# Products with the identity between the tiles of a hybrid attention and expert kernel: items with a bank of their own, or work in the bank the next item claims

## What is computed

```
x = x + attn_a(layernorm(x))   # 16 heads; groups of 64 rows, local keys + 64 cluster keys
x = x + ffn(layernorm(x))      # router, top-1 of 8 experts, y * max(probs)
x = x + attn_b(layernorm(x))   # 64 landmarks: kernel1 @ iterative_inv(kernel2) @ (kernel3 @ v)
x = x + ffn(layernorm(x))

def iterative_inv(K, n_iter=6):
    V = jnp.swapaxes(K, -1, -2) / denom
    for _ in range(n_iter):
        KV = K @ V
        V = 0.25 * V @ (13.0 * I - KV @ (15.0 * I - KV @ (7.0 * I - KV)))
    return V
```

## Time and profile before

| what | value |
|---|---|
| median of 3 runs | 1086.68 us (1081.27 to 1087.15) |
| profiled execution: span from its first to its last instruction | 1121.9 us |
| what lies around the span in that execution | not shown; span against the median of the runs: 35.2 us more |
| mean granted TensorE clock | 0.925 of full |
| TensorE busy / weight loads | 933.2 us (83%) / 666.9 us (59%) |
| VectorE, ScalarE, GpSimd busy | 831.1 (74%), 641.6 (57%), 472.3 us (42%) |

### The profile page before, as it was taken

How to read it: one execution, slowest core, us unless ns; L and a number is a source line. 1 busy time by engine, 2 the same in 40 slices (tenths; PEclk the granted TensorE clock), 3 DMA queues, 4 the chain that set the end, 5 groups by cost and what they waited for, 6 DMA issues and landing times. The chain is left out here.

```text
span 1121.9 us, 37263 instructions
## 1 busy us (share of the span) xinstructions
PE 933.2 (83%) x15213; PEld 666.9 (59%) x15213; DVE 831.1 (74%) x2089; ACT 641.6 (57%) x1387; POOL 472.3 (42%) x443
## 2 busy tenths in 40 slices
PE   7899989998989888677888986597689989772898
PEld 5567667675766665456566665454466666552653
DVE  3899899888557996567776687878487898685556
ACT  2456656782664574456667585356376776382630
POOL 2355345227356630445524156512543454446421
PEclk8899989999999999888999998689789999895999
DMA  9700000002321100120101101100311110102533
GB/s 319 254 3 3 4 2 3 3 3 95 115 72 58 31 8 13 38 68 12 49 21 52 41 12 35 30 29 2 102 42 50 39 46 20 49 26 90 160 105 99
DMA packets 51079, 61.71 MB, mean 55 GB/s; under 512 B 5601, under 2 KB 46177, under 8 KB 50913
## 3 DMA queue, kind: packets, MB, share of 16 engines
q1 hardware_dynamic: 43584, 42.51, 11.8%
q0 software_dynamic: 5760, 15.74, 4.4%
q10 hardware_dynamic: 1568, 1.09, 0.3%
HBM read 29.70 MB, written 29.62 MB: 53 GB/s over the span
## 5 line engine op out<-in xcount | busy, mean ns | idle before, releaser
L764 POOL TENSOR_TENSOR a_pr<-a_pr,a_smax 128x512 f32<-128x512 f32 x128 | 133.3, 1042 | 177.5 <-DVE a_smax L877 168.0
L1267 POOL TENSOR_TENSOR b_tm<-b_aw,b_sq 128x640 f32<-128x640 f32 (+1 forms) x48 | 65.4, 1362 | 148.9 <-ACT b_sq L1505 143.5
L871 DVE TENSOR_TENSOR a_pr<-a_bank,a_mask 128x512 f32<-128x512 f32 x128 | 82.8, 682 | 42.0 <-PE a_bank L1066 34.7
L963 ACT ACTIVATE a_pr<-a_pr 128x512 f32<-128x512 f32 x128 | 78.6, 630 | 51.9 <-POOL a_pr L764 44.1
L1247 POOL TENSOR_TENSOR b_pa<-b_pa,b_amax 128x512 f32<-128x512 f32 x64 | 67.1, 1048 | 70.3 <-ACT b_pa L1470 61.8
L969 ACT ACTIVATE a_pT<-a_bank 128x512 f32<-128x512 f32 x128 | 71.1, 596 | 41.2 <-PE a_bank L1075 30.0
L1075 PE MATMUL a_bank<-ident,a_pr 128*128 128x128 f32 x512 | 76.4, 289 | 20.2 <-ACT a_pr L963 17.6
L1256 POOL TENSOR_TENSOR b_pa<-b_pa,b_asum 128x512 f32<-128x512 f32 x64 | 66.7, 1043 | 58.4 <-DVE b_asum L1371 54.2
L307 POOL DMA_INDIRECT rows_sorted<-f_rows,f_pos x60 | 58.2, 969 | 72.2 <-DVE f_pos L403 53.8
L1398 DVE SCALAR_TENSOR_TENSOR b_aw<-b_tm,b_inverse 128x320 f32<-128x320 f32 (+1 forms) x144 | 63.4, 440 | 33.1 <-PE b_inverse L1646 13.7
L318 POOL DMA_INDIRECT f_rows<-results_sorted,f_pos x60 | 58.6, 977 | 66.9 <-issue 34.4
(11 more groups left out here) (238 smaller groups left out, 2359.8 us busy)
## 6 DMA issues: line engine op xcount, KB each, us to landing
f_xg<-rows_sorted SPq DMA_DIRECT2D x42, 256.0 KB, 3.2
results_sorted<-f_yg SPq DMA_DIRECT2D x42, 256.0 KB, 2.3
rows_sorted<-f_yg SPq DMA_DIRECT2D x2, 2944.0 KB, 18.5
X<-in_x SPq DMA_DIRECT2D x7, 512.0 KB, 11.0
out<-X SPq DMA_DIRECT2D x7, 512.0 KB
experts_w<-in_e_wT SPq DMA_DIRECT2D x2, 1024.0 KB, 9.3
rows_sorted<-f_rows,f_pos POOLq DMA_INDIRECT x60
f_rows<-results_sorted,f_pos POOLq DMA_INDIRECT x60
```

The source lines that it names most:

```text
L764: nc.gpsimd.tensor_tensor(out=pr[:, u % AHEAD], in0=pr[:, u % AHEAD], in1=smax[:, u % AHEAD, :].unsqueeze(2).broadcast_to([P, HQ, KEYS]), ...
L871: pre.emptied(V_.tensor_tensor(out=pr[:, u % AHEAD], in0=gb[:].rearrange("p (h k) -> p h k", h=HQ), in1=mask[:, u // 4, :].unsqueeze(1).br ...
L963: nc.scalar.activation(pr[:, u % AHEAD], pr[:, u % AHEAD], ACT.Exp, scale=float(HD) ** -0.5)\
L1267: nc.gpsimd.tensor_tensor(out=tm[:, a:b, k], in0=aw3[:, a:b, k], in1=sq[:, a:b, k], op=ALU.subtract).then_inc(s_tm, 1)
```

## The change

The 24 idle items leave both tables. In 91 places of the TensorE lists (28 and 63) stands a new item `warmN_name` instead, with N from 1 to 47, 424 products in all (143 and 281). It is no item of the ring: it claims the bank that the item `name` will claim and issues N products of the identity with itself into it, with no semaphore. `name` stands right behind it or, in places, a few items later (`3.warm7_ta3 3.R3.0 ... 3.ta3`). Everything else keeps its order, but since the idle items took places in the ring, nearly every item now gets another bank. The ring's turns had also kept apart some reads and writes that no semaphore did; seven waits are written out for them.

```
+def warm(nc, pe, ring, n, item, ident):
+    count, name = item[4:].split("_", 1)
+    gb = ring.claim(pe, n, name)
+    for _ in range(int(count)):
+        nc.tensor.matmul(gb[:, 0:P], ident[:], ident[:], start=True, stop=True)
...
 def claimed(entries, experts):
     for n, x in entries:
+        if x.startswith("warm"):
+            continue
...
                 elif item == "xn":                      # VectorE, first attention
+                    if n > 0:
+                        pre.filled_bank(dve, n - 1, "xT1")
+                        pre.filled_bank(dve, n - 1, "xb")
...
                 elif item in ("v0", "v1"):              # VectorE
+                    wait_later(dve, s_pv, (n - 1) * UNITS)
...
                 elif item.startswith("norm"):           # VectorE
+                    if n * NT + t >= 2:
+                        pre.filled_bank(dve, (n * NT + t - 2) // NT, f"yT{(t - 2) % NT}")
...
                 elif item in ("k0", "k1"):              # ScalarE
+                    if n >= 2:
+                        pre.filled_bank(act, n - 2, f"score{UNITS - 1}")
...
                 elif item == "vcl":                     # ScalarE
+                    wait_later(act, s_pv, (n - 1) * UNITS)
...
             def body(item, n, par):                     # TensorE, both attentions
+                if item.startswith("warm"):
+                    warm(nc, pe, pre, n, item, ident)
+                    return
...
-                if item.startswith("idle"):
-                    pre.filled(mm(gb[:, 0:P], ident[:], ident[:], start=True, stop=True), n, item)
-                    mm(gb[:, 0:P], ident[:], ident[:], start=True, stop=True)
-                    pre.emptied(mm(gb[:, 0:P], ident[:], ident[:], start=True, stop=True), n, item)
-                    return
...
                 elif item in ("v0", "v1"):              # TensorE, both attentions
+                    pre.brought_out(pe, n, ["xT0", "xT1"], item)
...
                 elif item == "xn":                      # VectorE, second attention
+                    if n > 0:
+                        ring.filled_bank(dve, n - 1, "xT1")
...
                 elif item == "d":                       # TensorE, second attention
+                    pe.wait_ge(s_k2, (n + 1) * 7)
...
 CLUSTER_ORDER = {
     "pe": """
-        0.idle0 0.idle1 1.idle0 0.xT0 0.xT1 1.idle1 0.lc 2.idle0 0.q0 0.k0 0.k1 0.wT 0.q1 0.xb 0.v0 0.xbT 0.ckv 0.v1
+        0.warm47_xT0 0.xT0 0.xT1 0.warm2_lc 0.lc 0.q0 0.k0 0.k1 0.wT 0.q1 0.warm1_xb 0.xb 0.v0 0.xbT 0.warm3_ckv
```

More of the change, by code:

```diff
@@ L1518, in body @@
             def body(item, n, par):
+                if item.startswith("warm"):
+                    warm(nc, pe, either, n, item, ident)
+                    return
                 if isinstance(n, str):
@@ L1523, in body @@
                 last = None
-                if item.startswith("idle"):
-                    ring.filled(mm(gb[:, 0:P], ident[:], ident[:], start=True, stop=True), n, item)
-                    mm(gb[:, 0:P], ident[:], ident[:], start=True, stop=True)
-                    ring.emptied(mm(gb[:, 0:P], ident[:], ident[:], start=True, stop=True), n, item)
-                    return
                 if item[:2] == "xT":
@@ L1542, in body @@
                 elif item in ("v0", "v1"):
+                    ring.brought_out(pe, n, ["xT0", "xT1"], item)
                     for j in range(2):
@@ new lines @@
+        m0.rx3.0 5.xbT m0.lt2 m0.rx3.1 4.weigh8 4.weigh9 4.weigh10 m0.lg3 4.weigh11 m0.lt3 4.yT1 5.ckv 5.v1 4.turn12
+        4.turn13 4.turn14 4.turn15 4.weigh12 4.weigh13 4.weigh14 4.weigh15 m0.s2 6.xT0 6.xT1 5.score0 6.lc 6.q0 6.k0
+        6.k1 4.pj1 4.yT2 m0.cT 6.wT 4.pj2 6.q1 6.xb 4.yT3 m0.warm1_bi0 m0.bi0 5.turn0 6.v0 6.xbT m0.bi1 4.pj3 6.ckv
+        6.v1 5.turn1 5.turn2 5.score4 5.turn3 m0.tt0 5.weigh0 5.weigh1 5.weigh2 5.weigh3 m0.tt1 m0.ty0 m0.tt2 m0.ty1
+        m0.ty2 m0.tt3 m0.tt4 5.turn4 5.turn5 5.turn6 m0.tt5 m0.ty3 m0.ty4 5.score8 m0.tt6 5.turn7 m0.ty5 m0.tt7
@@ new lines @@
+        0.sc4 0.warm13_sa0 0.sa0 0.tc4 0.tc5 1.q0 1.k0 0.w4 0.w5 0.tc6 0.tc7 0.w6 0.w7 1.warm2_q1 0.R0.0 1.q1 1.k1
+        1.v0 1.v1 1.S20 1.S21 1.S22 1.warm1_sc0 1.sc0 0.ta0 0.warm6_ta1 0.ta1 0.warm2_ta2 0.N0.0 0.ta2 1.S23 1.tc0
+        1.tc1 0.sa4 0.R1.0 1.w0 1.w1 m1.tt0 m1.tt1 m1.ty0 1.tc2 1.tc3 1.kT 1.warm1_sc4 0.N1.0 1.sc4 1.w2 1.d 0.R2.0
+        2.xT0 0.N2.0 1.tc4 1.w3 2.xT1 1.w4 1.tc5 m1.tt2 m1.ty1 0.R3.0 m1.tt3 0.ta3 1.tc6 1.w5 1.A 1.tc7 0.N3.0 0.ta4
+        1.w6 1.w7 0.R4.0 0.ta5 0.ta6 m1.tt4 0.N4.0 1.sa0 0.warm1_ta7 0.R5.0 0.ta7 m1.ty2 m1.ty3 0.N5.0 m1.ty4 0.Z
@@ new lines @@
+        5.sc4 m2.warm4_tt2 4.N1.0 m2.tt2 m2.ty0 m2.ty1 m2.tt3 m2.tt4 4.R2.0 5.tc4 m2.ty2 5.tc5 4.ta3 6.xT0 6.xT1
+        m2.tt5 5.w4 5.w5 4.N2.0 4.ta4 4.ta5 m2.ty3 4.R3.0 4.ta6 5.sa0 5.warm1_tc6 4.N3.0 5.tc6 m2.ty4 m2.tt6 5.kT 5.d
+        4.R4.0 m2.tt7 m2.ty5 4.ta7 4.N4.0 m2.ty6 5.A 4.R5.0 m2.tt8 m2.tt9 5.tc7 m2.ty7 m2.ty8 m2.tt10 4.N5.0 5.w6
+        5.w7 4.Z 5.R0.0 4.sv0 4.sv1 m2.tt11 5.ta0 4.pj0 4.pj1 4.pj2 4.pj3 6.q0 6.k0 6.q1 6.k1 6.v0 5.ta1 5.ta2 6.sc0
+        5.N0.0 m2.ty9 m2.ty10 m2.ty11 m2.tt12 5.R1.0 5.sa4 6.v1 5.N1.0 6.S20 6.S21 6.S22 6.tc0 m2.tt13 6.tc1 m2.ty12
@@ new lines @@
+        m2.tt14 5.R2.0 6.w0 6.w1 6.tc2 6.tc3 6.sc4 m2.warm4_ty13 5.N2.0 m2.ty13 m2.ty14 6.w2 6.w3 m2.tt15 6.tc4 6.tc5
+        6.S23 5.R3.0 5.ta3 m2.tt16 6.w4 6.w5 m2.tt17 m2.ty15 5.ta4 5.ta5 5.ta6 5.N3.0 6.kT 6.sa0 6.warm1_tc6 5.R4.0
+        6.tc6 m2.ty16 6.d 5.N4.0 m2.ty17 6.tc7 5.warm1_ta7 5.R5.0 5.ta7 6.A 6.w6 6.w7 m2.warm1_tt18 5.N5.0 m2.tt18
+        m2.tt19 m2.tt20 5.warm2_Z 5.Z 6.R0.0 m2.bi0 5.sv0 5.sv1 6.ta0 6.ta1 6.N0.0 6.ta2 m2.ty18 6.warm1_sa4 6.R1.0
+        6.sa4 m2.ty19 m2.tt21 6.N1.0 m2.tt22 5.pj0 5.pj1 7.xT0 6.R2.0 m2.bi1 7.xT1 5.pj2 5.pj3 6.N2.0 7.q0 6.R3.0
```

147 lines of the change are left out of this document (69 added, 78 removed).

## The result

The changed kernel takes 1088.8 us (median of 20 runs, 1085.9 to 1092.8), the kernel before 1084.5 (20 runs, 1073.8 to 1090.9): ratio 1.0058, interval 1.0035 to 1.008. It is slower, by 4.3 us in the medians and 6.3 by the ratio, where I had forecast 6.5 us faster. The profiled execution took 1088.86 us.

A forecast was written before the change was run, and what follows sets the result against it. No engine was always busy; whichever of TensorE (83%) and VectorE (74%) was behind set the end. Terms 0.9 + 2.5 - 4.2 - 4.0 - 0.7 - 1.0 = -6.5 us, applied to the median, gave 1080 us, range 1069 to 1093.

The forecast's parts named there:

- Removed ... I cost it at nothing: Taking out 24 idle items (72 products, 16 us of TensorE's time) costs nothing; what it could give is at most 1 us.
- Term 1, the start: 47 products before the first transposes delay the first projection to 16.6 to 17.6 us; cost 0.8 to 1.9, taken as 0.9.
- Term 2, groups without a gap: Products in blocks 2, 3, 7 and the last inverse, among others, that no wait covers; cost 0 to 7.4 us, taken as 2.5.
- Term 3, the hand-over: From block 3 to 4, Z, sv and three pj run at full clock; gain 0 to 4.6 us, taken as 4.2.
- Terms 4 to 6: Half-clock time going: five stretches gain 4.0 us, those at 36.5 and 159.4 us 0.7, two inverses 1.0.
- VectorE takes it back: Rival: TensorE's waits grow by the time freed, half the hand-over gain remains; sum +1.3, put at 1086 us, chance 0.27.
- TensorE's busy time up by little: Sign expected across the kernel: products fill what matmuls at half clock took before, so TensorE's busy time hardly rises.
- The slower rival: Products get stuck beside indirect DMAs in the last inverse, deciding from about 0.4 us each; +7.4, 1094 us, chance 0.16.
- The added waits: Each waits for something that happened long before in the trace, so they cost nothing unless such a lead is eaten up.
- the late signals: Delays beside indirect DMAs at 798 to 811, 964 to 972 and 1022.52 to 1032.23 us; no term was said to rest there.
- term 6: Two inverses at 698.7 and 1012.7 us lose half-clock time; gain 0 to 4 us, taken as 1.0.
- the fast rival: TensorE is behind nearly everywhere, so the half-clock gains reach their upper ends; -18.4 us, 1068 us, chance 0.17.

The follow-up runs named there:

- f2: Kernel before without its 24 idle items, each item's bank as in the changed kernel, no added waits or products; ratio 1.0029.
- f3: Kernel before with its 72 idle products cut from 128 columns to 1, banks, waits and order kept; ratio 1.0036.
- e1: Changed kernel with all 91 groups of products taken out, idle items still gone, new waits in; ratio to the kernel before 1.0037.
- h5: Kernel before with added waits, no new products, and without the 12 idle items of the first stage; ratio 1.0059.
- f1: Kernel before with the added waits alone, idle items, banks and order as before, no new products; ratio 1.0011.
- h4: Kernel before with added waits; second stage as in the changed kernel (its 12 idle items gone, 281 products in); ratio 1.0021.
- g3: Kernel before with idle items kept, added waits, and the 281 products of the second stage alone; ratio 0.9974.
- h6: Kernel before with idle items kept, added waits, and only the 212 second-stage products that have a gap; ratio 0.9967, 1080.2 us.
- e2: Changed kernel without the 47 products at the start alone; ratio to the kernel before 1.0082.
- h1: Kernel before with idle items kept, added waits, and the 47 products at the start alone; ratio 1.0079.
- e3: Changed kernel without the groups that have no gap to fill, 95 products less; ratio to the kernel before 1.0033.
- h2: Kernel before with idle items kept, added waits, and only the 26 first-stage products that have no gap; ratio 1.0051.
- g4: Kernel before with idle items kept, added waits, and 23 products alone at the hand-over from block 3 to block 4; ratio 0.997.
- g1: Kernel before with idle items kept, added waits, and only the 282 of 424 products that have a gap; ratio 0.9972.
- f4: Changed kernel, with its 424 products and waits, with the 24 idle items put back where they stood; ratio to the kernel before 1.004.

## Why the prediction was wrong

**The step that failed first: "Removed ... I cost it at nothing".** I had bounded it at 1 us. The 24 idle items are worth 3 to 4 us by f2, f3 and e1, each with an interval of about 3.5 to either side (h5 for the first stage alone 6, 5 against f1). I had looked at whether they stood in gaps and whether a bank was waited for. What they gave was clock; at which places is argued and not shown: the kernel before has them at 163, 383 to 391 and 415 us, and two of the changed kernel's half-clock stretches (171.1 to 177.9, 420.2 to 423.6) begin a few us behind such a place. f3 shows that it was their work, since it changes nothing but the columns (ratio 1.0036, 1.0004 to 1.0069). And that their 144 records move the edges of the program blocks I did not know.

**The unforeseen term: a halt for instructions, +5.5 us in the profile.** Inserted instructions can cost more than their duration. They moved an edge of a program block into N5 of block 1, on the chain of the inverse, with half clock behind it (18.1 against 12.6 us). That this stretch loses time by the halt is well supported: the lost time stands in nine profiles with the halt and in none of eleven without. What it is worth in the time of the kernel is not shown: h4 has it and is 5 us behind g3, which has not, but h6 has it too (16.6 us) and is the fastest of all. A kernel that only shifts the edges, with nothing else changed, was not run.

**Term 1, the start: mechanism right, size off.** Transposes at 14.95 and first projection at 17.39 lie in the ranges given. But I took 0.9 us, near the low end, and against the same profile it is 1.65. In that profile the clock rose at 16.0; in the second it rose at 13.1 and the projections began at 14.55, so the price is 2.8 at the first projection and 2.3 at score4; alone, beside the idle items, 5.5 us (h1). Yet e2, which starts without the 47 products, is no faster: what it wins there it loses again from turn7 of block 7 on.

**Term 2, groups without a gap: +2.5, measured in part.** e3 against the changed kernel gives 2.7 us by the ratios, h2 against f1 4.3 us for 26 products of 5.8 us. h2's profile, however, loses 5.0 us at the halt near N5 again and 3.9 at the change of stage. I can't separate the products' own time from where they push the edges.

**Term 3, the hand-over: right where it stands, not shown in the whole.** Z, sv and pj last what the forecast said. The stretch takes 23.1 us in the changed kernel, 24.8 in f1, 26.5 and 29.3 in the two profiles of before: the clock's fall there varies in place, and the first profile had its dearest form. So it wins 1.7 to 6.2 us, for a forecast of 4.2. In the timed runs g4 has 3.2 us (ratio 0.9943 to 0.9997), which fits; but g1 and h6, whose profiles do not win here (26.2 and 26.0 us), have the same.

**Terms 4 to 6: the half-clock time went, the gain did not come.** 61 us are left where I had said 90. Of -5.7 us I find nothing that the timed runs set apart: g3 has 41 us of half clock, g4 111.7, and they are equally fast. The rival "VectorE takes it back" had this right. Its own sum, +1.3, gives 1088.0; the 1086 that it was put at counted on luck. It names only a part of the reason: from 731 to 906 us nearly all kernels keep one pace, with 6.8 to 20.5 us of half clock and with 78 products or none, and in the last inverse the pace of R2 comes from GpSimd. Who sets it elsewhere no run tells. "TensorE's busy time up by little", one of the signs, failed as well: it rose by 50 us against the first profile and 67 against the second.

**The slower rival was not what happened.** It had the right side and nearly the size (1094), by a mechanism that is absent: 0.24 us a product. The added waits cost nothing, as forecast.

**The sum** was made on a profile 35 us over the timed runs. I had seen that and applied the terms to the median; but also their bounds came from its stretches, and a second profile has half clock at other places (16 stretches for 25). The statement that no term rests on the late signals was wrong for term 6. There are slips too: the low ends of terms 3 to 6 add up to 21.4 and not 21.8, which makes the fast rival 1068.7; and VectorE's share in these stretches goes down to 48% (13.11 of 27.30 us) and 55% (7.56 of 13.70), not to 66%. Neither moves the forecast. What the runs show is which terms were wrong, and not a new sum: the losses of single parts, put together, come to more than the changed kernel loses.

## What to carry to other kernels

Time at half clock is no cost by itself, and filling all of it brought nothing here: 23 products at one hand-over gave a ratio of 0.997, 212 to 282 gave no more, and all 424 in place of the idle items gave 1.0058. Begin with the one or two stretches where several half-clock items stand on a chain, and measure before adding more. Work that seems idle may be what holds the clock up: cut its columns to one before you remove it, as f3 does, and see what it was worth. Before you add or remove many instructions on TensorE, look for halts "<-issue" in the middle of an item and for packets on the instruction queue beside them: inserted work moves the edges of program blocks through everything behind it. And take a second profile of the kernel before, if the first is longer than its timed runs.

## What the runs showed of the hardware

- TensorE's program arrives in packets of 16,384 bytes, one for every 122 to 128 matmul records. Each of the halts of 1.1 to 2.2 us in the middle of an item that I followed in the changed kernel (8 of them, 12.1 us in sum) has a packet that began 2.3 to 2.9 us before TensorE went on and ended 1.3 to 1.5 before. The kernel before has 9 of them in its second profile (0.8 to 2.2 us, 11.6 in sum), all in the first stage, five of them in weigh, whose 32 to 128 small matmuls run off in about a microsecond.
- Such a halt can pull the clock down: 596.27 to 597.93 idle, at half clock from 597.70 to 608.00 although TensorE was busy for 10.00 of the 10.30 us. It need not: behind five of the eight halts of the changed kernel (112.1, 120.0, 216.2, 307.0 and 339.0 us) no half clock follows.
- The granted clock of the profiled execution and the median time are hardly related between kernels: 0.949 and 1079.5 us (g4), 0.981 and 1078.8 (g3), 0.979 and 1088.1 (f4), 0.944 and 1089.9 (h1).
